# Attention with quantised heads before a routed expert block: sixteen small operations per tile moved from VectorE to GpSimd, and a ninth head written as bytes

## The chip, the cores and the metric

The kernel runs on one core of a Trainium2 chip. Its engines are TensorE (PE, the matrix engine), VectorE (DVE), ScalarE (ACT, activations such as the exponential), GpSimd (POOL) and SyncE (SP, which here only issues transfers). Each engine works through its own list of instructions in order; they wait for each other by semaphores. The metric is the device time of one execution in microseconds, the median of several.

## The reference

Two residual layers over x of 2 x 512 tokens with 512 channels. The first is cross attention to 2048 context rows with 16 heads of 32 channels, in which queries, keys, values and probabilities are rounded to whole numbers of a scale ("fake quantisation"):

```
q = (x @ Wq + bq) * scale ; k, v = split(cond @ Wkv + bkv)
q = _fq_sym(q, axis=-1) ; k = _fq_sym(k, axis=-1) ; v = _fq_sym(v, axis=2)
attn = softmax(einsum('bhqd,bhkd->bhqk', q, k), axis=-1)
attn = _fq_unsigned(attn, axis=-1)      # round(attn / (max/255)) * (max/255)
x = x + einsum('bhqk,bhkd->bhqd', attn, v) @ Wp + bp      # x was normalised before q
```

The second layer routes every token by a gate to some of 8 experts (a gated network each) and adds their weighted sum. The rounded probability of a key is round(255 * exp(s - max s)), a whole number from 0 to 255. The kernel computes just that: the exponential with the bias ln 255 - max s, written as an integer.

## The kernel before

**Stages.** Context rows, keys, values and queries are made and rounded first (to about 133 us). Then comes the attention over eight tiles i = 0 to 7 of 128 queries, each with 16 heads h; a position in it is written as "head h of tile i". A short tail follows (last projection, norm, gate, lists of tokens), then the experts. The change is all in the attention.

**One head** runs through the engines so:
- TensorE (`scores`) multiplies the queries with the 2048 keys, in two halves of 1024 in PSUM.
- VectorE *stages*: it multiplies with the negative step and writes to one of four `staged` buffers (h % 4), with the minimum of each row as an accumulated result. Even heads go in one operation over 2048 columns (`stage_whole`, L1258), odd heads in two over 1024 (`stage_half`, L1267). Then `make_bias` turns the minimum into the exponential's bias in `exp_bias`: for an even head `s_low + LN255` (L1278), for an odd one `min(s_low, s_first) + LN255` (L1276), 128 x 1 numbers each. In VectorE's list the bias of an odd head stands behind the whole staging of the next one, and the bias of an even head behind the first half of the next one.
- ACT takes the exponential (L946) of the staged scores. Even heads are written as bytes, odd heads as 16-bit words; the sum of the row comes along.
- SP issues a DMA transpose (L453), so that keys lie along the partitions. Of words that is 2048 columns; of bytes 1024, as two neighbouring bytes are turned as one 16-bit word.
- For a byte head POOL then takes the pairs apart (`unpack`, L632, a cast from bytes to 16-bit numbers). A word head needs nothing.
- TensorE multiplies with the values (`values`, L1639): in the slot of each even head h, heads h - 5 and h - 6.

**What sets the order.** Every engine's list is written out by hand. VectorE may stage a head when the exponential four heads before is done. ACT needs the bias, and for writing its result the transpose four heads before to have landed. An unpacking needs its transpose to have landed and the values of the head four before to be done.

**What else runs in a tile.** Between the heads stand: the attention result scaled and cut into two 16-bit parts by POOL (`attention_half`, L617 to L624) and transposed by SP (`transpose_attention`); the projection of the tile before by TensorE in four pieces at heads PROJECT_AT (L1521), which ACT takes at head 11 (L934) and POOL adds to x (`add_rows`, L639 to L643); the variance of the tile before that (L917 on ACT), its square root by nine small operations on POOL (`deviation`, L650 to L659), the normalised rows (L922, L928 on ACT, `rows_low` L664 on POOL), and their transpose and stores by SP (`store_rows`, `keep_rows`, `add_to_output`). POOL also copies the next queries into place (`next_queries`, L596). SP loads a piece of the expert weights per tile (`load_piece`). Where one of POOL's small operations needs the one before, it waits for its semaphore.

## Time and profile before

| | us |
|---|---|
| median of 3 runs | 745.07 (744.51 to 746.85) |
| the profiled execution | 742.73 |
| its span, first to last instruction | 740.9 |
| VectorE busy | 573.1 (77%) |
| ScalarE busy | 461.5 (62%) |
| GpSimd busy | 371.5 (50%) |
| TensorE busy | 623.8 (84%) |

The busy shares are means over stages with different limits, so they have to be read by stretches: the page cuts the span into 40 slices of 18.5 us. "Busy" counts instructions that compute; waits, register work and the issue of transfers aren't in it. A POOL instruction's row ends when its result is there; on VectorE and ACT the next instruction can start a little before the row of the last has ended.

### The profile page before, as it was taken

The page shows a single profiled execution, that of the slowest core. Times are in us where ns is not written, and L with a number is a line of the kernel's source. Part 1 is how long each engine was busy: PE and PEld are TensorE (multiplying, and loading weights), DVE is VectorE, ACT ScalarE, POOL GpSimd, SP SyncE. Part 2 cuts the span into 40 slices and gives each one's busy share as a digit, 9 for nine tenths or more (in the row PEclk, how much of TensorE's full clock was granted, in tenths as well). Part 3 has the DMA queues.
Part 4 walks back from the last instruction along what each step waited for, and adds up shares of the span by engine and source line. Part 5 has one row for each costly group of instructions (what it writes and reads, how often), then busy time and mean ns, then how long its engine had stood idle before and what let it go on. Part 6 is the DMA issues. An engine that isn't in the chain of part 4 may idle for free. (4 is left out here: it accounts for less than half of the span.)

```text
span 740.9 us, 15739 instructions
## 1 busy us (share of the span) xinstructions
PE 623.8 (84%) x5298; PEld 325.9 (44%) x5298; DVE 573.1 (77%) x974; ACT 461.5 (62%) x552; POOL 371.5 (50%) x394
## 2 busy tenths in 40 slices
PE   6999999566777777777767687799999999999993
PEld 2444443233434343343434355455555555555551
DVE  4997778999999999999999996784746537455330
ACT  6334358688899999999999997243434435344321
POOL 5254457544666675757576754215334453343503
PEclk9999999999999999999999999899999999999997
DMA  7767767999999999999999995459895887977804
GB/s 246 195 150 168 167 142 124 189 170 179 181 171 191 211 174 213 174 217 181 206 180 210 188 201 107 133 178 183 223 250 127 235 220 184 254 137 213 149 6 57
DMA packets 325908, 131.25 MB, mean 177 GB/s; under 512 B 300901, under 2 KB 300901, under 8 KB 325865
## 3 DMA queue, kind: packets, MB, share of 16 engines
q1 hardware_dynamic: 318688, 114.48, 71.5%
q0 software_dynamic: 7168, 16.26, 10.6%
q8 instruction: 19, 0.31, 0.2%
q14 instruction: 25, 0.20, 0.1%
q10 hardware_dynamic: 8, 0.01, 0.0%
HBM read 44.33 MB, written 12.06 MB: 76 GB/s over the span
## 5 line engine op out<-in xcount | busy, mean ns | idle before, releaser
L946 ACT ACTIVATE work<-spare,exp_bias 128x2048 int16<-128x2048 f32 (+1 forms) x128 | 255.5, 1996 | 32.0 <-DVE exp_bias L1276 30.4
L1267 DVE TENSOR_SCALAR_CACHE_REDUCE spare<-psum,q_step_now 128x1024 f32<-128x1024 f32 x128 | 162.2, 1274 | 0.1
L632 POOL CAST work<-work 128x2048 int16<-128x2048 uint8 x63 | 119.1, 1890 | 81.8 <-DMA work<-work 67.5
L1258 DVE TENSOR_SCALAR_CACHE_REDUCE spare<-psum,q_step_now 128x2048 f32<-128x2048 f32 x64 | 150.4, 2350 | 0.1
L1679 PE MATMUL psum<-keys_region,work 128*128 128x512 f16 x256 | 73.1, 383 | 52.1 <-DVE spare L1267 28.9
L1679 PE MATMUL psum<-keys_region,bias_hl 128*128 128x512 f16 x256 | 71.9, 382 | 32.1 <-DVE spare L1267 28.3
L737 POOL DMA_INDIRECT work<-x_rows,slot_tok x32 | 50.1, 1564 | 97.1 <-DVE slot_w L1453 73.8
L749 POOL DMA_INDIRECT out_dram<-keys_region,slot_tok x32 | 51.7, 1617 | 74.1 <-ACT keys_region L1025 67.1
L1521 PE MATMUL psum<-work,spare 128*128 128x480 f16 (+1 forms) x396 | 79.2, 360 | 0.9 <-DVE work L1426 0.9
L1521 PE MATMUL psum<-work,keys_region 128*128 128x480 f16 x384 | 78.9, 366 | 0.0
L1639 PEld LDWEIGHTS psum<-values_region,work 128*128 128x128 f16 x2048 | 67.4, 96 | 24.2 <-DMA work<-work 12.5
L1639 PE MATMUL psum<-values_region,work 128*128 128x32 f16 x2048 | 70.5, 176 | 3.6 <-DMA work<-work 3.4
L1475 DVE SCALAR_TENSOR_TENSOR resid<-resid,psum 128x480 f32<-128x480 f32 x32 | 20.7, 648 | 58.8 <-ACT resid L1015 58.8
L1679 PEld LDWEIGHTS psum<-keys_region,work 128*128 128x128 f16 x256 | 16.7, 97 | 95.8 <-DVE spare L1267 59.5
L1008 ACT ACTIVATE query_region<-resid 128x480 f16<-128x480 f32 x32 | 19.3, 603 | 61.3 <-DVE resid L1478 61.3
L1521 PEld LDWEIGHTS psum<-work,spare 128*128 128x128 f16 x396 | 38.3, 98 | 39.0 <-ACT work L1036 1.0
L1521 PEld LDWEIGHTS psum<-work,keys_region 128*128 128x128 f16 x384 | 37.3, 98 | 39.5
L1679 PEld LDWEIGHTS psum<-keys_region,bias_hl 128*128 128x128 f16 x256 | 17.9, 97 | 72.5 <-DVE spare L1267 57.9
L1025 ACT ACTIVATE keys_region<-psum,slot_w 120x512 f32<-120x512 f32 x32 | 21.2, 686 | 43.8 <-PE psum L1521 38.0
L1521 PE MATMUL psum<-query_region,work 128*128 128x512 f16 x192 | 44.8, 379 | 3.7 <-issue 2.8
L563 POOL TENSOR_TENSOR values_region<-values_region 128x512 f16<-128x512 f32 x16 | 21.6, 1349 | 50.1 <-ACT values_region L845 50.1
L1015 ACT ACTIVATE resid<-psum 128x480 f32<-128x480 f32 x32 | 18.2, 570 | 43.6 <-PE psum L1521 43.6
(222 smaller groups left out, 1014.0 us busy)
## 6 DMA issues: line engine op xcount, KB each, us to landing
spare<-in_L_ffn_Wd_dram SPq DMA_DIRECT2D x8, 1024.0 KB, 15.6
spare<-in_L_ffn_Wg_dram SPq DMA_DIRECT2D x7, 1024.0 KB, 5.7
spare<-in_L_ffn_Wu_dram SPq DMA_DIRECT2D x7, 1024.0 KB, 12.1
work<-in_ctx_dram SPq DMA_DIRECT2D x3, 1024.0 KB, 5.7
work<-work SPq DMA_TRANSPOSE x181, 3.6
token_region<-in_L_xattn_Wkv_dram SPq DMA_DIRECT2D x2, 1024.0 KB, 6.9
resid<-in_x_dram SPq DMA_DIRECT2D x2, 1024.0 KB, 8.7
x_rows<-work SPq DMA_DIRECT2D x8, 256.0 KB, 2.3
```

The lines of the kernel that those rows point to most:

```text
L563: nc.gpsimd.tensor_tensor(k_cut[b][:, :, 1, :], k_deq[b], k_cut[b][:, :, 0, :], ALU.subtract).then_inc(k_cut_ready[b], 1)
L632: nc.gpsimd.tensor_copy(p_T_int[h % 4 // 2], pair_bytes[h % 4 // 2]).then_inc(unpacked, 1)
L737: nc.gpsimd.indirect_dma_start(x_sel[par][:, t, :], None, x1_rows, bass.IndirectOffsetOnAxis(ap=slot_tok[par][:, t:t + 1], axis=0)).then_i ...
L749: nc.gpsimd.indirect_dma_start(out_rows, bass.IndirectOffsetOnAxis(ap=slot_tok[par][0:ROWS, t:t + 1], axis=0), y_out[0:ROWS, t, :], None, ...
L946: nc.scalar.activation(last_int[h % 2] if words and h >= H - 2 else p_int[h % 4], scores, ACT.Exp, bias=exp_bias[:, h % 4:h % 4 + 1], scal ...
L1025: nc.scalar.activation(y_out[0:ROWS, t, :], bank(4 + t % 3)[0:ROWS, :], ACT.Copy, scale=slot_w[par][0:ROWS, t:t + 1]).then_inc(y_ready[t % ...
L1258: nc.vector.tensor_scalar(staged[h % 4], psum[:, at:at + 4, :].rearrange("p b k -> p (b k)"), q_step_now[:, h:h + 1], None, ALU.mult, ALU.min,
L1267: nc.vector.tensor_scalar(staged[h % 4][:, 1024 * c:1024 * c + 1024], psum[:, at:at + 2, :].rearrange("p b k -> p (b k)"), q_step_now[:, h ...
L1475: own.link(nc.vector.scalar_tensor_tensor(gate_1[f % 2], tanh_g[f % 2], 1.0, bank(f % 2)[:, 0:PASS], ALU.add, ALU.mult))
L1521: ins = nc.tensor.matmul(out, lhs(a, c), rhs(b, c), start=start and n == 0, stop=stop and n == len(terms) - 1)
L1639: ins = nc.tensor.matmul(bank(6 + n)[:, at:at + HD], p_T[h % 4][:, t, :], v_int[:, t, h * HD:h * HD + HD], start=t == 0, stop=t == KT - 1)
L1679: ins = nc.tensor.matmul(bank(at + piece), q_now[h // HQ][:, h % HQ, :], key_parts[:, h // 2, 1024 * c + 512 * piece:1024 * c + 512 * piec ...
```

## The change

1. In tiles 1 to 7 the biases are made by POOL, head by head, as the first thing of each head's turn; only tile 0 and the last two heads of tile 7 stay with VectorE, under a semaphore of their own (`edge_bias`). VectorE's loop over the tiles 1 to 7 becomes tile 1, a loop over 2 to 6, and tile 7.
2. POOL's list for a tile is written anew around the biases: one other task between each two of them. The unpacking of head h - 3 follows the bias of the odd head h; the square root is done in two parts (after the biases 2 and 6).
3. Head 9 is written as bytes too (nine of sixteen heads, `BYTE_HEADS`), transposed in pairs and unpacked by POOL behind the bias of head 12. The buffers' views are made for all four places instead of two, and the counts of `unpacked` are 9 a tile.
4. ACT's work between the heads moves: normalising the rows from head 4 to 7, cutting them from 5 to 8, the squares from 13 to 15. In SP's list the first half of the attention is transposed at head 1 of the next tile instead of behind head 15, the second at 5 instead of 4; x1 is stored at head 2 and the rows at 10, where all three transfers stood at head 7; the weights' piece goes from 10 to 12.
5. PROJECT_AT goes from (8, 10, 10, 12) to (10, 10, 12, 12).
6. The semaphore `tri_ready` is merged into `const_ready`.

```diff
-PROJECT_AT = (8, 10, 10, 12)
+PROJECT_AT = (10, 10, 12, 12)
+BYTE_HEADS = (0, 2, 4, 6, 8, 9, 10, 12, 14)
...
             def transpose_tile(i, first, after_rows, count=H):
...
-                    if h == 10 and i < QT - 1 or first and h == 6:
+                    if h == 12 and i < QT - 1 or first and h == 6:
...
-                    if h == 4 and not first:
+                    if h == 1 and not first:
+                        transpose_attention(i - 1, 0)
+                    if h == 5 and not first:
                         transpose_attention(i - 1, 1)
-                    if h == count - 1:
+                    if h == count - 1 and count < H:
                         transpose_attention(i, 0)
-                    if h == 7 and after_rows:
+                    if h == 2 and after_rows:
+                        add_to_output(i - 2)
+                    if h == 10 and after_rows:
                         store_rows(i - 2)
...
+            def make_bias(i, h):
+                pool.wait_ge(scores_taken, 2 * H * i + 2 * h + 2)
+                passed()
+                at = slice(h % 4, h % 4 + 1)
+                if h % 2:
+                    nc.gpsimd.tensor_scalar(exp_bias[:, at], s_low[:, at], s_first[:, at], LN255, ALU.min, ALU.add).then_inc(bias_made, 1)
+                else:
+                    nc.gpsimd.tensor_scalar(exp_bias[:, at], s_low[:, at], LN255, None, ALU.add).then_inc(bias_made, 1)
...
             def attention_tile(i, after_rows, following):
...
+                if not following:
+                    add_at, half_at = 12, 13
+                else:
+                    add_at, half_at = 14, 15
+                for h in range(H if following else H - 2):
+                    make_bias(i, h)
+                    if h == 0:
+                        pool.wait_ge(unpacked, unpacked_earlier(i, 0))
+                        passed()
+                        next_queries(i, 1)
+                    if h == 1:
+                        unpack(i - 1, 14)
+                    if h == 2 and after_rows:
+                        scale = deviation_begun(i - 2)
+                    if h == 4:
+                        attention_half(i - 1, 1)
+                    if h == 6 and after_rows:
+                        deviation_ended(i - 2, scale)
+                    if h == 8 and following:
...
+                        next_queries(i + 1, 0)
+                    if h == 10 and after_rows:
+                        rows_low(i - 2)
...
+                    if h == 12:
+                        unpack(i, 9)
+                    if h % 2 and 3 <= h < 15:
+                        unpack(i, h - 3)
+                    if h == add_at:
+                        add_rows(i - 1)
+                    if h == half_at:
+                        attention_half(i, 0)
                 unpack(i, 12)
...
-                    words = h % 2 or not following and h == H - 2
+                    words = h not in BYTE_HEADS or not following and h == H - 2
...
-                    if h == 4 and after_rows:
+                    if h == 7 and after_rows:
                         normalise_rows(i - 2)
-                    if h == 5 and after_rows:
+                    if h == 8 and after_rows:
                         cut_rows(i - 2)
...
-                    if h == 13 and not first and following:
+                    if h == 15 and not first and following:
                         square_rows(i - 1)
...
-            def attention_tile(i, first):
+            def attention_tile(i, first, after_first=False, last=False):
                 for h in range(0, H, 2):
                     stage_whole(i, h, first)
-                    if h:
+                    if first and h:
                         make_bias(i, h - 1)
-                    elif not first:
-                        make_bias(i - 1, H - 1)
+                    if after_first and h == 0:
+                        make_bias(0, H - 1)
...
                     stage_half(i, h + 1, 0, first)
-                    make_bias(i, h)
+                    if first or last and h == H - 2:
+                        make_bias(i, h)
                     stage_half(i, h + 1, 1, first)
```

How the lists stand, in the instructions of the built programs. Lines are those of each program; `spare` holds the staged scores, `s_low` and `s_first` the minima, an operation over 2048 columns is a whole staging, one over 1024 a half, and REGISTER_ALU and ISA rows only work out what a wait compares with.

VectorE in a tile of the loop, before, a whole staging and the two halves behind it:

```order
L1258 TENSOR_SCALAR spare,s_low<-psum,q_step_now 128x2048
L1276 TENSOR_SCALAR exp_bias<-s_low,s_first 128x1
L1265 REGISTER_ALU
L1267 TENSOR_SCALAR spare,s_first<-psum,q_step_now 128x1024
L1278 TENSOR_SCALAR exp_bias<-s_low 128x1
L1265 REGISTER_ALU
L1267 TENSOR_SCALAR spare,s_low<-psum,q_step_now 128x1024
```

and the same place now:

```order
L1312 TENSOR_SCALAR spare,s_low<-psum,q_step_now 128x2048
L1301 REGISTER_ALU
L1319 REGISTER_ALU
L1321 TENSOR_SCALAR spare,s_first<-psum,q_step_now 128x1024
L1319 REGISTER_ALU
L1321 TENSOR_SCALAR spare,s_low<-psum,q_step_now 128x1024
```

Both biases are gone from it, and the stagings follow each other.

POOL in the second half of a tile of the loop, before: the unpacking of head 8, the rows added, the unpacking of head 10, and the attention's first half:

```order
L632 CAST work<-work 128x2048
L639 ISA
L639 TENSOR_TENSOR x_mean<-proj_sum,row_sum 128x1
L640 ISA
L640 TENSOR_TENSOR work<-work,resid 128x512
L75 ISA
L643 TENSOR_SCALAR x_mean<-x_mean 128x1
L630 REGISTER_ALU
L632 CAST work<-work 128x2048
L611 ISA
L614 REGISTER_ALU
L617 TENSOR_TENSOR work<-work,p_rsum 128x256
```

and now, from the bias of head 10 to the unpacking of head 8 behind bias 11 and that of head 9 behind bias 12:

```order
L659 TENSOR_SCALAR exp_bias<-s_low 128x1
L699 TENSOR_TENSOR work<-work 128x512
L653 REGISTER_ALU
L657 TENSOR_SCALAR exp_bias<-s_low,s_first 128x1
L645 REGISTER_ALU
L648 REGISTER_ALU
L650 CAST work<-work 128x2048
L653 REGISTER_ALU
L659 TENSOR_SCALAR exp_bias<-s_low 128x1
L648 REGISTER_ALU
L650 CAST work<-work 128x2048
```

Every task of POOL now has a bias ahead of it and one behind, and there is one unpacking more.

## Rows read from the trace of the kernel before

**Rows 1.** The page's slices: VectorE's busy tenths in 40 slices of 18.5 us.

```profile
DVE  4997778999999999999999996784746537455330
```

**Rows 2.** Busy us in one stretch: PE, its weight loads, DVE, ACT, POOL; clock, DMA.

```profile
289.00:328.00 39.00, 28.90 (x384) 15.60 (x384) 39.00 (x67) 35.74 (x44) 26.17 (x33) 1.00 0.98 194
```

**Rows 3.** VectorE in order of time: start, us, engine, line, operation, tiles.

```profile
307.58 1.28 DVE L1267 TENSOR_SCALAR_CACHE_REDUCE spare<-psum,q_step_now 128x1024 f32<-128x1024 f32 x1
...
308.78 2.35 DVE L1258 TENSOR_SCALAR_CACHE_REDUCE spare<-psum,q_step_now 128x2048 f32<-128x2048 f32 x1
...
311.05 0.22 DVE L1276 TENSOR_SCALAR exp_bias<-s_low,s_first 128x1 f32<-128x1 f32 x1
311.18 1.28 DVE L1267 TENSOR_SCALAR_CACHE_REDUCE spare<-psum,q_step_now 128x1024 f32<-128x1024 f32 x1
...
312.38 0.16 DVE L1278 TENSOR_SCALAR exp_bias<-s_low 128x1 f32<-128x1 f32 x1
312.44 1.28 DVE L1267 TENSOR_SCALAR_CACHE_REDUCE spare<-psum,q_step_now 128x1024 f32<-128x1024 f32 x1
...
313.64 2.35 DVE L1258 TENSOR_SCALAR_CACHE_REDUCE spare<-psum,q_step_now 128x2048 f32<-128x2048 f32 x1
...
320.90 0.20 DVE L1218 RECIPROCAL p_rsum<-p_sum 128x8 f32<-128x8 f32 x1
...
359.95 0.20 DVE L1218 RECIPROCAL p_rsum<-p_sum 128x8 f32<-128x8 f32 x1
```

**Rows 4.** POOL's groups from 250 to 406 us (four tiles), then rows by time.

```profile
L632 POOL CAST work<-work 128x2048 int16<-128x2048 uint8 x32 | 60.5, 1890 | 35.0 <-DMA work<-work 29.7 <-POOL bias_hl L596 2.0 <-PE psum L1639 1.4
...
L596 POOL COPY work<-query_region 64x512 f16 x8 | 4.9, 608 | 3.3 <-PE psum L1679 2.3 <-POOL work L596 1.0
...
L654 POOL TENSOR_SCALAR ln_t<-ln_y,ln_var 128x1 f32<-128x1 f32 x12 | 4.1, 341 | 2.5 <-POOL ln_y L655 1.7 <-POOL ln_y L651 0.8
...
L659 POOL TENSOR_SCALAR x_mean<-x_mean,ln_y 128x1 f32<-128x1 f32 x4 | 1.0, 260 | 0.4
...
305.13 0.62 POOL L617 TENSOR_TENSOR work<-work,p_rsum 128x256 f32<-128x256 f32 x1
...
307.10 1.89 POOL L632 CAST work<-work 128x2048 int16<-128x2048 uint8 x1
...
325.67 0.21 POOL L643 TENSOR_SCALAR x_mean<-x_mean 128x1 f32<-128x1 f32 x1
325.94 1.89 POOL L632 CAST work<-work 128x2048 int16<-128x2048 uint8 x1
```

**Rows 5.** ACT's exponentials in the same four tiles, and one by time.

```profile
L946 ACT ACTIVATE work<-spare,exp_bias 128x2048 int16<-128x2048 f32 x32 | 64.0, 2001 | 13.1 <-DVE exp_bias L1276 12.7
L946 ACT ACTIVATE work<-spare,exp_bias 128x2048 uint8<-128x2048 f32 x32 | 63.7, 1991 | 0.0
...
311.30 2.00 ACT L946 ACTIVATE work<-spare,exp_bias 128x2048 int16<-128x2048 f32 x1 [0.25 <-DVE exp_bias L1276]
```

**Rows 6.** SP's waits in four tiles; landing of one byte and one word head.

```profile
SPq L314 <- ACT work L946: 7.3, 13, 0.9
...
DMA to landing us min/median/max: 3.3/3.3/3.3
...
DMA to landing us min/median/max: 4.3/4.3/4.3
```

**Rows 7.** TensorE in the slot of head 10, tile 4, in order of time.

```profile
313.79 0.60 PE L1679 MATMUL psum<-keys_region,bias_hl 128*128 128x512 f16 x2 [0.66 <-DVE spare L1267]
...
315.26 1.50 PE L1521 MATMUL psum<-work 128*128 128x128 f16 x24
316.59 1.46 PE L1679 MATMUL psum<-keys_region,bias_hl 128*128 128x512 f16 x6
```

**Rows 8.** The tail by stretches; the figure behind the five engines is the granted clock.

```profile
447.90:451.30 3.40, 3.40 (x30) 2.80 (x28) 2.59 (x5) 3.10 (x6) 2.27 (x3) 0.51 0.85 199
...
471.80:475.20 3.40, 3.40 (x25) 1.68 (x24) 2.69 (x15) 0.00 (x0) 0.89 (x1) 0.50 0.00 0
```

134 lines of the change are left out of this document (69 added, 65 removed).

## Prediction, made before the changed kernel ran

> **What bounds the kernel now.** I read the page's slices first [rows 1]: VectorE is busy 9 tenths or more from slice 8 to slice 24, and that stretch, the attention over eight tiles of 128 queries, is where all edits lie. The table by stretches [rows 2] has VectorE busy for 39.00 us of every 39.00 us, ScalarE (ACT) 35.7, GpSimd (POOL) 26.2, TensorE 28.9. The same reciprocal of two tiles starts at 320.90 and 359.95 [rows 3]: one tile takes 39.05 us, and VectorE sets it. The chain of waits is of no use here; it names TensorE in the expert stage, which nothing touches. So the questions are what VectorE gives up, and who is next.
>
> Three others stand close behind. ACT sat idle for 13.1 us before the exponentials in four tiles [rows 5]: 3.3 a tile, so it needs 35.8. The SP queue waited 7.3 us in the same four tiles [rows 6]: 1.8 a tile, so it is occupied for 37.2. POOL waited 29.7 us for transposes to land and 2.3 + 1.4 for TensorE [rows 4], 8.35 a tile: what it must do takes 39.05 - 8.35 = 30.7, its own short gaps included.
>
> **VectorE: what it gives up.** The tile's biases stand in its stream twice per pair of heads. From one pair [rows 3]: the staging of the even head starts at 308.78, the bias L1276 at 311.05, the next staging at 311.18, the bias L1278 at 312.38, the staging behind it at 312.44. So a bias costs 0.13 us and 0.06 us from start to start, although the rows give 0.22 and 0.16 as their length, since the next instruction starts while it ends. Stagings that follow each other with no bias (312.44 to 313.64) already run in 1.20, so nothing else changes between them. Before, there are 128 biases; after, VectorE keeps the 16 of tile 0 and the last two of tile 7. 110 go, 55 of each kind: 55 x 0.13 + 55 x 0.06 = 10.45 us. A whole tile: 39.05 - 8 x 0.19 = 37.5.
>
> The rule that speaks of this price is in the Trainium skill, VectorE: DVE Perf Modes, section "The DRAIN you can't avoid": the next VectorE operation does not begin until the pipe is empty. Read so, each bias would cost its full row, and 55 x (0.22 + 0.16) = 20.9 us would go; the starts in the rows, which overlap the rows' ends, contradict it here.
>
> **GpSimd: what it takes on.** Per whole tile 16 biases and one more unpacking. A bias of an even head has the form of L643 (one operation with a constant), 0.21; one of an odd head that of L659 (a pointer and a constant), 0.260 [rows 4]. Behind such a short operation the next starts 0.06 us after its end (325.67 + 0.21 to 325.94 [rows 4]); I take 0.07. So 8 x 0.28 + 8 x 0.33 = 4.9. The unpacking of head 9 is a row of L632, 1.89. Sum: 30.7 + 4.9 + 1.9 = 37.5 us a tile, the same as VectorE's. The cover is gone: POOL has no spare time, and every wait in its stream is paid. A bound from below: the biases hide in their neighbours as on VectorE (0.13 and 0.06), which makes 34.1. From above: L654's 0.341 with its 0.21 of waiting for itself, 0.55 a bias, makes 41.4. I take the middle form since a bias waits for VectorE and not for POOL's own last result.
>
> A bias stands behind what POOL does for the head before. Longest is the turn of the tile: after bias 15, three operations of the attention's half (305.13 to 307.10, 2.0 [rows 4]) and an unpacking (1.9) stand ahead of bias 0, which then comes 4.2 us after bias 15 where the stagings come 2.3 apart: 1.9 late. Who waits: ACT's exponential of head 0. But an exponential may start late, as staging buffer h is taken again only four heads on: three intervals of 2.34 less the 2.0 of the exponential, 5.0 us. Today ACT starts it up to 2.4 us after the staging ended, since the bias of an odd head stands behind the next whole staging (half from 307.58, bias 311.05, exponential 311.30 [rows 3, 5]). POOL can be 2 us late and still be no later than now; per head it catches up some 0.1 to 0.2.
>
> The new wait: the unpacking of head h stands behind bias h + 3 and ahead of bias h + 4. It needs the exponential (2.0), the issue of the transpose and 3.3 us to its landing [rows 6]: 5.5 after bias h, against 7.0 for three heads. The spare 1.5 goes where ACT also norms and cuts the rows (heads 7 and 8) and POOL has no unpacking between two biases (head 10): there, for the unpackings of 8 and 9, I count 0.4 us of waiting a tile. So POOL's turn is 37.9, 0.4 over VectorE's for the five tiles 2 to 6: 1.9 us, of which tile 7 (no queries to fetch for a next one, 2 x 0.61 and their gaps [rows 4]) gives some back: **1.3 lost**. Bounds 0 and 3.
>
> **TensorE.** The projections move from heads 8, 10, 10, 12 to 10, 10, 12, 12: two slots with 24 small matmuls instead of one. In such a slot [rows 7] the 24 start at 315.26 and the scores behind them at 316.59; the first two of these six are through at about 316.59 + 1.46/3 = 317.08. VectorE's second half was started at 317.31 and would now be at 313.64 + 2.27 + 1.20 = 317.11. Nothing is left; I take 0.05 us in two slots of seven tiles: **0.7 lost**. Bounds 0 and 2.8 (0.2 a slot, by the 0.15 between a staging's end and the scores that it frees).
>
> **SP and ACT.** The issues stay as many; head 9's is half as large, the att transposes, the store of x1 and that of the rows are spread over heads 1, 2, 5, 10. SP's 37.2 becomes 37.2 less what a smaller transpose saves: the landing of a word head took 4.3 us from issue, that of a byte head 3.3, so up to 1 less. 36.2 to 37.2 fits under 37.9, hidden. ACT's exponential is as long for bytes as for words (1991 and 2001 ns), 35.8 fits too. Cost nothing, but with 0.7 and 1.7 us of cover left.
>
> **After the attention.** After the last exponential the tail (last probabilities, projection, norm, gate) and the experts shift as a whole. In the tail TensorE's granted clock falls to half for 3.4 us at 447.9, at 471.8 and once between [rows 8]. Where those stretches lie will change; TensorE is at the limit in about half of them, so 1.5 us either way, which I put into the range.
>
> **Sum.** -10.45 + 0.7 + 1.3 = -8.45 us. The profiled execution took 742.73 (span 740.9), 2.3 below the median of 745.07; its span would be 732.5. The time of the median kind: 745.07 - 8.45 = **736.6**.
>
> **Rivals.**
> - *GpSimd is the bound at a gain*: landings come later than counted, a turn of 38.5. Five tiles gain 0.55 each and the tiles 1 and 7 1 us each: 4.7 us less, 740.4 (738.5 to 743). For it: 37.5 is a sum of many short rows, and POOL cannot recover a wait. Against: before, the landings were ahead of it by 7.4 us a tile. Chance 0.20.
> - *Slower*: the same place, POOL between bias h + 3 and h + 4, above 39.05 us a tile. It decides from 1.5 us a tile more than my 37.5, which is 0.1 us on each bias or a 0.2 us wait at each of the nine unpackings. At 39.6 five tiles lose 0.55 each and the two others about 0.5: +3.3, 748.4. For it: the loop unpacking, bias, exponential, transpose, unpacking feeds back into itself. Chance 0.11. The Trainium skill, GPSIMD Engine Reference, section 4.1 "Engine selection", advises against it: two-input elementwise work is about twice as slow on GpSimd as on VectorE. With twice VectorE's rows (0.43, 0.31, and 0.07 each) the biases would cost 7.0 and the turn would be 39.6, this rival's number; the rows of like form (0.26 and 0.21 against 0.22 and 0.16) show 1.2 to 1.4 times.
> - *Nothing gained*: VectorE's 0.19 a pair turns into waiting for scores, as TensorE's order would be the bound: 745, within 0.3%. Against: between stagings TensorE waits for VectorE [rows 7], and a slot of the dear kind takes 4.3 us (313.79 to 318.05) of 4.67. Chance 0.07.
> - *Better than the sum*: no loss on POOL and TensorE and a good clock in the tail: 733 to 734. Chance 0.06.
> - The forecast itself, 734.5 to 738.5: 0.56.
>
> Faster by over 0.3% (2.2 us, about what a measurement of this kernel tells from no change): 0.56 + 0.06 + 0.16 of the first rival = 0.78. Slower by over 0.3%: 0.11. The rest, 0.11, within. The range 733.0 to 743.5 leaves out the slower rival and the edges.
>
> **What would show it.** Right: in tiles 2 to 6 the same reciprocal comes every 37.5 to 37.9 us; VectorE has no bias but staging after staging, idle under 0.5 us a tile; POOL is busy for about 33 of 37.7 us with waits for DMA below 1 us a tile. The first rival: VectorE idle on exponentials, POOL waiting for landings 1 us a tile. The third: VectorE idle on TensorE. Wrong altogether if the period falls and the span doesn't: then the tail took it back.

## The result, and the profile after

The changed kernel takes 749.46 us (median of 5 runs, 748.18 to 751.12), the kernel before on the same chip 744.79 (744.51 to 746.85): a ratio of 1.0061, 95% interval 1.0040 to 1.0082. It is slower by 0.6%, a small difference that the interval separates from none. 736.6 had been forecast, and 749.46 lies outside 733.0 to 743.5. Of the rivals the slower one happened: GpSimd (POOL) above 39.05 us a tile.

The profiled execution of the changed kernel has a span of 748.9 us, that of before 740.9. These 8.0 us lie between two single executions; the medians differ by 4.7. First a tile by stretches; the columns are those of [rows 2].

```profile
331.10:370.57 39.47, 28.25 (x384) 15.21 (x384) 37.92 (x53) 35.85 (x43) 32.52 (x50) 1.00 0.94 186
```

VectorE did give up its time: 37.92 busy of 39.47 us, where [rows 2] has 39.00 of 39.00. But the tile is longer. From the first staging of a tile to that of the next (on VectorE) tiles 0 to 6 took 40.61, 39.80, 38.75, 41.08, 38.36, 39.47 and 39.35 us; before, tile 0 took 38.86, tile 1 39.24 and the others 39.04 to 39.05. So the five middle tiles together are 1.8 us longer, and tile 0, in which VectorE still makes the biases, 1.75. These 1.75 can't be called a price of the change: with the same tile 0 experiment 2 and three of the four versions in experiment 10 took 38.86 for it, the fourth 40.18. Here TensorE's granted clock lay at half from 132.1 to 138.9 us. What VectorE waited for between 140 and 450 us (us in total, times, the longest):

```profile
DVE spare L1321 <- PE psum L1736: 9.4, 15, 1.5
DVE spare L1312 <- PE psum L1736: 2.5, 5, 0.5
```

It stood 11.9 us waiting for scores, more than the 10.45 us that its biases had cost. TensorE issues scores behind values, and waited in its turn for what the values need, and ACT for biases:

```profile
PE psum L1696 <- DMA work<-work: 19.6, 28, 2.0
...
ACT work L1000 <- POOL exp_bias L659: 13.7, 22, 1.8
ACT work L1000 <- POOL exp_bias L657: 13.5, 21, 1.1
PE psum L1696 <- POOL work L650: 9.4, 8, 1.8
```

One waiting leads to the next: staging waits for scores, these stand behind values, values wait for a landing or an unpacking, these come late since the exponential was late, and that waited for its bias on POOL. Here is POOL from one adding of the rows (L667) to the next, in order of time, answering to the rows by time in [rows 4]:

```profile
331.05 1.27 POOL L667 TENSOR_TENSOR work<-work,resid 128x512 f32<-128x512 f32 x1
...
339.13 0.30 POOL L657 TENSOR_SCALAR exp_bias<-s_low,s_first 128x1 f32<-128x1 f32 x1 [0.37 <-POOL bias_hl L614]
339.71 1.89 POOL L650 CAST work<-work 128x2048 int16<-128x2048 uint8 x1 [0.28 <-DMA work<-work]
...
344.01 0.30 POOL L657 TENSOR_SCALAR exp_bias<-s_low,s_first 128x1 f32<-128x1 f32 x1 [0.37 <-POOL ln_y L675]
344.37 1.89 POOL L650 CAST work<-work 128x2048 int16<-128x2048 uint8 x1
346.35 0.22 POOL L659 TENSOR_SCALAR exp_bias<-s_low 128x1 f32<-128x1 f32 x1
346.91 0.62 POOL L635 TENSOR_TENSOR work<-work,p_rsum 128x256 f32<-128x256 f32 x1 [0.34 <-ACT work L950]
...
365.75 1.89 POOL L650 CAST work<-work 128x2048 int16<-128x2048 uint8 x1
367.73 0.30 POOL L657 TENSOR_SCALAR exp_bias<-s_low,s_first 128x1 f32<-128x1 f32 x1
368.09 1.89 POOL L650 CAST work<-work 128x2048 int16<-128x2048 uint8 x1
...
370.51 1.27 POOL L667 TENSOR_TENSOR work<-work,resid 128x512 f32<-128x512 f32 x1
```

From 331.05 to 370.51 are 39.46 us; I call this POOL's turn. The two waits for another engine or a transfer that it shows (0.28 and 0.34) are all there are in it. So POOL's own work with its own gaps is 38.9 us a turn, where the forecast had 37.5. The unpackings (1.89) and the stagings (2.35 and 1.27) are as long as before, so POOL's added work does not lengthen VectorE's operations, nor its own. A bias is 0.30 or 0.22 long, and four of the eight odd ones stand 0.36 to 0.37 us behind a result of POOL's own.

The attention's last exponential starts later too. First the kernel before, then the changed one:

```profile
447.29 1.99 ACT L946 ACTIVATE work<-spare,exp_bias 128x2048 int16<-128x2048 f32 x1
```

```profile
452.58 2.00 ACT L1000 ACTIVATE work<-spare,exp_bias 128x2048 int16<-128x2048 f32 x1 [0.38 <-DMA work<-work]
```

5.3 of the 8.0 us between the two spans are lost by here; 2.7 more behind it. The latter is no clear price of the change either: from the last exponential to the end it took 293.6 us before and 296.3 here, and 293.7 to 297.8 in the other versions below, none of which alters anything there. In the tail TensorE's granted clock lay at half (1.2 of 2.4 GHz) for 13.6 us in one piece, answering to the separate 3.4 us of [rows 8]:

```profile
470.00:483.60 13.60, 11.72 (x95) 6.12 (x94) 10.30 (x46) 2.56 (x5) 2.25 (x3) 0.50 0.19 67
```

### The profile page after: what moved, and what is told of

It reads as the page before. It is cut to its first block, busy times and chain, and to the rows that moved or that the text cites. A ratio compares the mean times of both kernels' runs of the same rounds, so it can differ in the third digit from the quotient of the medians.

```text
span 748.9 us, 15883 instructions
## 1 busy us (share of the span) xinstructions
PE 630.3 (84%) x5298; PEld 328.7 (44%) x5298; DVE 566.1 (76%) x864; ACT 462.1 (62%) x552; POOL 419.9 (56%) x512
## 4 chain that ended last, share of the span: by engine, by line
PE 50%; issue 15%; DMA 8%; DVE 7%; SPq 7%; ACT 5%; POOL 5%; POOLq 1%; another core or an unknown queue 1%; ACTq 0%; DVEq 0%
PE psum L1578 45%; DMA work<-work 8%; ACT work L1000 4%; SPq L467 3%; DVE spare L1321 2%; POOL work L650 2%; SPq L435 2%; SPq L465 2%; DVE spare L1312 1%; PE psum L1583 1%; PE psum L1793 1%; PE psum L1875 1%; PE psum L1787 0%; POOL exp_bias L657 0%
## 5 line engine op out<-in xcount | busy, mean ns | idle before, releaser
L1000 ACT ACTIVATE work<-spare,exp_bias 128x2048 uint8<-128x2048 f32 (+1 forms) x128 | 255.5, 1997 | 37.0 <-POOL exp_bias L659 13.7
L1321 DVE TENSOR_SCALAR_CACHE_REDUCE spare<-psum,q_step_now 128x1024 f32<-128x1024 f32 x128 | 160.3, 1273 | 9.6 <-PE psum L1736 9.4
L650 POOL CAST work<-work 128x2048 int16<-128x2048 uint8 x71 | 134.2, 1892 | 27.8 <-DMA work<-work 15.7
L783 POOL DMA_INDIRECT work<-x_rows,slot_tok x32 | 52.6, 1644 | 97.7 <-DVE slot_w L1510 73.0
L1736 PE MATMUL psum<-keys_region,work 128*128 128x512 f16 x256 | 76.6, 411 | 34.6 <-DVE spare L1321 19.2
L1696 PE MATMUL psum<-values_region,work 128*128 128x32 f16 x2048 | 71.3, 177 | 32.6 <-DMA work<-work 22.6
L1696 PEld LDWEIGHTS psum<-values_region,work 128*128 128x128 f16 x2048 | 65.9, 96 | 61.1 <-DMA work<-work 41.0
L1578 PEld LDWEIGHTS psum<-work,keys_region 128*128 128x128 f16 x384 | 37.3, 98 | 39.5
L1736 PEld LDWEIGHTS psum<-keys_region,work 128*128 128x128 f16 x256 | 19.3, 102 | 77.6 <-DVE spare L1321 47.1
L1736 PEld LDWEIGHTS psum<-keys_region,bias_hl 128*128 128x128 f16 x256 | 19.4, 98 | 59.2 <-DVE spare L1321 44.4
```

What stands on the lines that cost most here:

```text
L650: nc.gpsimd.tensor_copy(p_T_int[h % 4], pair_bytes[h % 4]).then_inc(unpacked, 1)
L783: nc.gpsimd.indirect_dma_start(x_sel[par][:, t, :], None, x1_rows, bass.IndirectOffsetOnAxis(ap=slot_tok[par][:, t:t + 1], axis=0)).then_i ...
L1000: nc.scalar.activation(p_out, scores, ACT.Exp, bias=exp_bias[:, h % 4:h % 4 + 1], scale=-1.0, accum_out=p_sum[:, h:h + 1]).then_inc(exp_do ...
L1321: nc.vector.tensor_scalar(staged[h % 4][:, 1024 * c:1024 * c + 1024], psum[:, at:at + 2, :].rearrange("p b k -> p (b k)"), q_step_now[:, h ...
L1578: ins = nc.tensor.matmul(out, lhs(a, c), rhs(b, c), start=start and n == 0, stop=stop and n == len(terms) - 1)
L1696: ins = nc.tensor.matmul(bank(6 + n)[:, at:at + HD], p_T[h % 4][:, t, :], v_int[:, t, h * HD:h * HD + HD], start=t == 0, stop=t == KT - 1)
```

## Experiments

Diffs are against the changed kernel. "Turn" is the time between two starts of L667 in the middle tiles.

**1. Nine unpackings halved.** From tile 1 on POOL unpacks only one byte of each pair (the rest of the conversion is left out).

```
-nc.gpsimd.tensor_copy(p_T_int[h % 4], pair_bytes[h % 4])
+nc.gpsimd.tensor_copy(p_T_int[h % 4][:, 0:1], pair_bytes[h % 4][:, 0:1])   # tile 0: whole
```

> The changed kernel, but from tile 1 on each unpacking takes apart only one byte of each pair (half the columns), so the probabilities of every second block of keys are stale; all else is the same. POOL's work falls by about 8 x 0.9 = 7 us a tile. Theory P (POOL's own work of about 39 us a tile sets the pace of tiles 2 to 6 in the changed kernel, through late biases, late exponentials and late values): a tile takes 37.5 to 37.9 us, the waits of VectorE for scores nearly vanish, and the time is 9 to 14 us below the changed kernel's 749.5, 736 to 741. Theory S (the two slots with 24 projection matmuls hold the scores up): the waits before the second halves of heads 11 and 13 stay at 0.6 us each, a tile takes 38.7 or more, the time falls by under 3 us. Theory C (the new order of SP's and ACT's work): also under 3 us.

Measured: 734.78 us, ratio to before 0.9893 (0.9858 to 0.9927), turn 37.7 to 37.9. One tile by stretches:

```profile
320.00:357.80 37.80, 28.61 (x393) 15.80 (x389) 37.78 (x51) 35.73 (x43) 24.83 (x49) 1.00 0.99 195
```

VectorE is busy throughout, at 37.8 us: the forecast's 37.5 and a little. The two slots of TensorE with two projections cost nothing when the values are there on time. With POOL relieved the change is worth what it was meant to be (0.9893, where 736.6 against 745.07 is 0.9886), so the loss comes through POOL. The edit does two things at once, though: it takes 7.6 us of work from POOL, and it brings every byte head's values 0.85 us nearer to its landing. It can't tell POOL's load from the length of that way; experiments 4 and 7 bear on it.

**2. All biases back on VectorE**, in the changed layout, with head 9 as bytes.

```
 # VectorE, each tile (the odd heads' biases and ACT's waits likewise)
-                    if first or last and h == H - 2:
-                        make_bias(i, h)
+                    make_bias(i, h)
...
 # POOL, each head
-                    make_bias(i, h)
```

> The changed kernel's order on SP, ACT, POOL and TensorE and nine byte heads, but all biases on VectorE where they stood before. VectorE's need is 39.05 us a tile again, POOL's about 39.1 less 16 biases of 0.37 to 0.45, 32 to 33. Theory P: 39.05 a tile and no waits, 743.5 to 746, equal to before. Theories S and C (order or slots cost by themselves): slower than before, 747 to 752, with VectorE waiting for scores, and TensorE's clock falling inside the attention.

Measured: 744.43, ratio 1.0018 (1.0004 to 1.0032), turn 39.0 to 39.1. So the new order and the ninth byte head cost 0.2% by themselves at a VectorE that needs 39.05 us a tile; that they would cost as little at one that needs 37.5 is not shown by this run. Most of the loss came with the biases on POOL. In two turns POOL waited here:

```profile
POOL work L650 <- DMA work<-work: 9.3, 12, 1.5
POOL work L635 <- ACT work L949: 2.9, 2, 1.5
POOL work L650 <- PE psum L1689: 1.4, 3, 0.5
...
POOL bias_hl L614 <- PE psum L1729: 1.1, 2, 0.5
POOL work L614 <- PE psum L1729: 0.9, 2, 0.4
```

15.6 us in two, 7.8 a turn. To take all of this off (39.07 - 7.8 = 31.3) would be too much, because a part of it is there without any waiting for others. First a copy of queries and two unpackings in this run:

```profile
333.15 0.61 POOL L614 COPY bias_hl<-query_region 64x512 f16 x1 [0.54 <-PE psum L1729]
...
336.02 1.89 POOL L650 CAST work<-work 128x2048 int16<-128x2048 uint8 x1 [1.42 <-DMA work<-work]
...
340.15 1.89 POOL L650 CAST work<-work 128x2048 int16<-128x2048 uint8 x1 [0.50 <-POOL ln_y L675]
```

and the places of the first two before (the third row is the unpacking behind the other copies):

```profile
333.74 0.61 POOL L596 COPY bias_hl<-query_region 64x512 f16 x1 [0.45 <-POOL work L632]
...
335.71 1.89 POOL L632 CAST work<-work 128x2048 int16<-128x2048 uint8 x1 [0.51 <-POOL bias_hl L596]
...
354.37 1.89 POOL L632 CAST work<-work 128x2048 int16<-128x2048 uint8 x1 [0.42 <-POOL work L596]
```

The copy that waited 0.54 for TensorE stands 0.45 behind POOL's own unpacking anyway, and of the 1.42 for a landing 0.51 would be there too. Behind such results of POOL's own the two first copies and the two unpackings behind the copies stand 0.36 to 0.51 each, 1.7 us a turn, and the list waits for one more (L699) that no run here shows free of another wait. So POOL's own work without biases is about 33.0 us, 33.4 with the same 0.4 at L699. Sixteen biases bring it to 38.9: 5.5 to 5.9 us, 0.34 to 0.37 each. This is an estimate from these rows; whole waits taken off would give 7.6 us or 0.47 each.

**3. The projections at their old heads**, `PROJECT_AT = (8, 10, 10, 12)`.

> The changed kernel with the projections at heads 8, 10, 10, 12 as before. Theory S: the wait before the second half of head 13 goes, that of head 11 stays; 0.6 us a tile, 745 to 746. Theory P: the slot of head 8 has no slack for values that come late either, so the wait moves there; within 1.5 us of 749.5, or slower.

Measured: 768.16, ratio 1.0343 (1.0318 to 1.0368). VectorE waited 13.0 us for TensorE in 157 us, less than four of the turns of 42.4 to 42.8, and TensorE for the transposed attention:

```profile
DVE spare L1321 <- PE psum L1736: 13.0, 4, 4.3
...
PE psum L1578 <- DMA work<-work: 9.5, 3, 3.3
```

Since the second transpose of the attention now stands behind head 5, the first projection comes too early at head 8. The move was needed; it says nothing on the price of the double slots.

**4. Head 9 as words again**: `BYTE_HEADS` without 9, and its unpacking gone from POOL, 2 us a turn.

> The changed kernel with head 9 written as words again (eight byte heads, no unpacking behind bias 12), all else as changed. By theory P it takes 1.89 + 0.4 us off POOL's turn of about 39.1: 36.8 a tile, under VectorE's 37.5; a tile takes 37.5 to 38.0 and the time is 737 to 742, better than both kernels, unless the larger transpose (SP and DMA) takes its place: then 744 to 748 with POOL waiting for landings over 1 us a tile. Theory S: within 2 us of 749.5.

Measured: 748.28, ratio 1.0073 (1.0047 to 1.0098), turn 39.5 to 39.9. POOL was relieved of a whole unpacking and nothing came back. In four tiles it waited for the values of earlier heads, and 3.2 us for landings:

```profile
POOL work L650 <- PE psum L1692: 5.6, 3, 1.9
```

A tile:

```profile
331.10:370.80 39.70, 28.58 (x389) 15.19 (x388) 37.94 (x51) 35.85 (x44) 30.46 (x49) 1.00 0.97 192
```

POOL is busy for 30.46 us here, 2 less than in the changed kernel, and the tile is no shorter. So POOL's load alone does not set the turn.

**5. Head 9 as words and the other unpackings halved.**

> As the run with head 9 as words, and GpSimd unpacks only one byte of each pair from tile 1 on (this part of the probabilities' conversion is left out). GpSimd is then far from the bound. Theory D (with head 9 as words the transposes take 38.4 us of DMA time a tile, against 37.3 with it as bytes, and with the waits around them they are the next bound): tiles of 38.5 to 39.0 us, 740 to 744. Theory P alone (only GpSimd's work counts): as with nine byte heads, 37.8 us a tile, 734 to 737.

Measured: 740.24, ratio 0.9926 (0.9902 to 0.9951). A tile:

```profile
323.81:362.02 38.21, 28.98 (x384) 15.57 (x384) 37.76 (x51) 35.64 (x43) 23.77 (x48) 1.00 1.01 199
```

The DMA engines are busy all the time (1.01): with eight byte heads their transfers need about 38.2 us a tile, with nine (experiment 1) under 37.8. This bound stands in [rows 2] too, as the last but one figure, 0.98 of 39.00 us, and the prediction didn't use it. With eight byte heads it would have held the tile near 38.2 us, above VectorE's 37.5. The turn of experiment 4 lies 1.3 to 1.7 above 38.2, so this bound by itself doesn't explain that run.

**6. More throwaway matmuls**: four instead of two behind the values of each odd head, to see if the half clock inside the attention is a cause.

> The changed kernel with four instead of two throwaway matmuls behind the values of each odd head, so that TensorE waits less idly. Theory C (the stretches of 3.4 us at half clock inside the attention are a cause of the longer tiles): these stretches go or become rarer, tiles near 39.0, 744 to 747. Theory P (they are a consequence of waiting for GpSimd): 748 to 751, and the tiles stay at 39.4 in the mean or above, with the stretches at half clock or without.

Measured: 749.88, ratio 1.0052 (1.0033 to 1.0072), five stretches at half clock between 160 and 400 us as before. The filling came behind the wait, not into it, so this shows only that two more matmuls there neither help nor hurt.

**7. One unpacking halved, at four places.** A half unpacking takes 1.04 instead of 1.89 us, so the relief is 0.85 us a turn. Only the head differs:

```
+whole = slice(0, 2) if isinstance(i, int) and i == 0 or h != 9 else slice(0, 1)
-nc.gpsimd.tensor_copy(p_T_int[h % 4], pair_bytes[h % 4])
+nc.gpsimd.tensor_copy(p_T_int[h % 4][:, whole], pair_bytes[h % 4][:, whole])
```

> The changed kernel with the unpacking of head 9 alone cut to one byte of each pair from tile 1 on (that part of the conversion is left out): GpSimd is relieved by 0.95 us a tile, a ninth of what the run with all nine cut was relieved by. Theory P: slope one, tiles of 38.5 instead of 39.5 us, 742 to 744. If GpSimd's work were only one of several causes, or the loop of late landings the main one: 746 to 749.

> The changed kernel with the unpacking of head 4 alone cut to one byte of each pair from tile 1 on (that part of the conversion is left out). Same relief of GpSimd as in the run that cut head 9's, 0.95 us a tile, but at another place of its turn: head 4 is unpacked behind bias 7, where the exponentials' lag behind the stagings still climbs to its highest value at heads 8 and 9, head 9 behind bias 12, where it falls anyway and GpSimd only waits for the next landing sooner. Theory W (what counts is GpSimd's work between the turn of the tile and the peak of the lag): tiles of 38.4 to 38.8 us and 742 to 745.5, at least 2 us under the run that cut head 9's. Theory P in its simple form (GpSimd's sum over a tile counts, wherever it lies) and theory C (the half clock): the same as that run, 747 to 749.

> The changed kernel with the unpacking of head 0 alone cut to one byte of each pair from tile 1 on (that part of the conversion is left out): again 0.95 us a tile less for GpSimd, now behind bias 3, ahead of the biases 4 to 7. Theory R (rings: GpSimd's work of 38.9 us a tile is tied within some tenths with a path bias 7 - exponentials 7 to 10 - landing of head 10 - its unpacking, and with the SP queue, whose transposes of heads 2 to 6 follow each other without a pause): only a part comes back, a turn of 38.9 to 39.3 us and 743.5 to 746.5, ratio to before 1.001 to 1.005, better than both others since this place lies ahead of bias 7. If GpSimd's work alone decided: 38.5 us and 741 to 743. If nothing of so small a relief came back: 39.4 and 746 to 748.

> The changed kernel with the unpacking of head 2 alone cut to one byte of each pair from tile 1 on (that part of the conversion is left out): 0.95 us a tile less for GpSimd, as at heads 9, 4 and 0, now behind bias 5, where no path through ScalarE runs beside it. Theory R (one ring holds the turn at 39.4: bias 3 - exponential 3 - ScalarE's taking of the attention - GpSimd's half - bias 5 - bias 7 - exponentials 7 to 10 - landing of head 10 - unpacking - bias 15 - half - bias 0 - bias 3; the heads 0, 4 and 9 lie beside ScalarE's stretches of it, head 2 lies on it): the relief counts in full, a turn of 38.4 to 38.8 us, 742.5 to 745.5 where the kernel before takes 745, ratio 0.997 to 1.001. If a relief of this size is lost wherever it lies: 39.4 us, ratio 1.003 to 1.006.

| halved head | ratio to before (95%) | turns in tiles 3 to 5, us |
|---|---|---|
| none (changed kernel) | 1.0061 (1.0040 to 1.0082) | 39.42, 39.59, 39.46 |
| 9 | 1.0032 (1.0013 to 1.0050) | 39.04, 39.45, 39.43 |
| 4 | 1.0052 (1.0039 to 1.0065) | 39.17, 39.42, 39.40 |
| 0 | 1.0034 (1.0021 to 1.0047) | 39.26, 39.50, 39.48 |
| 2 | 1.0030 (1.0016 to 1.0044) | 39.18, 39.31, 39.35 |

Little of the 0.85 comes back, at no place: at most 0.4 us in a turn, mostly under 0.2. Over the six turns between the first and the last L667, 0.7 to 1.3 us of 5.1 come back. In each trace POOL stands at the next operation that needs another engine's result. Head 9 (the short unpacking, then the wait for head 10's landing):

```profile
363.12 1.04 POOL L651 CAST work<-work 128x1024 int16<-128x1024 uint8 x1
364.25 0.30 POOL L658 TENSOR_SCALAR exp_bias<-s_low,s_first 128x1 f32<-128x1 f32 x1
365.30 1.89 POOL L651 CAST work<-work 128x2048 int16<-128x2048 uint8 x1 [0.75 <-DMA work<-work]
```

Head 4, with the wait at the unpacking of head 6 (with head 2 halved it is 0.94 at the same place):

```profile
355.85 1.89 POOL L651 CAST work<-work 128x2048 int16<-128x2048 uint8 x1 [0.98 <-DMA work<-work]
```

Head 0, with the wait at the attention's half, for ACT's copy that follows exponential 3:

```profile
344.90 1.04 POOL L651 CAST work<-work 128x1024 int16<-128x1024 uint8 x1
346.02 0.22 POOL L660 TENSOR_SCALAR exp_bias<-s_low 128x1 f32<-128x1 f32 x1
347.44 0.62 POOL L635 TENSOR_TENSOR work<-work,p_rsum 128x256 f32<-128x256 f32 x1 [1.20 <-ACT work L951]
```

In the changed kernel POOL stands 0.06 to 0.34 us at the same places. So POOL's work is tied, within a few tenths, with the way from a bias over the exponential and the transpose (or ACT's copy) back to POOL, at several places of the turn. My theory of one place that counts (heads ahead of bias 7) fell with head 0 and again with head 2.

**8. Heads 2 and 12 halved.**

> The same with the unpacking of head 12 (behind the turn of the tile, ahead of bias 0) cut too: both lie on the ring of theory R, 1.9 us a tile. The ring would need 37.5, so VectorE's 37.5 to 37.8 us and the DMA engines' 37.3 hold the tile: 37.8 to 38.2 us, 737.5 to 741, ratio 0.990 to 0.995, as much as the run with all nine unpackings cut reached, with two. If lost wherever it lies: 39.0 us or more, ratio above 1.000.

Measured: 0.9987 (0.9973 to 1.0002), turns of 38.60, 38.64 and 38.52. Against head 2 alone that is 0.6 to 0.8 less a turn, 4.6 us over the six: the second relief, at head 12's unpacking ahead of bias 0 of the next tile, gave back most of its 0.85. Head 12 was not halved alone, so whether its place did it, or the two reliefs together, is not shown. The forecast of 37.8 to 38.2 failed here too.

**9. The SP queue.** First the second transpose of the attention halved besides head 4's unpacking (the low halves are not transferred):

```
-att_T[:, DK * n:DK * n + DK, :], att_hl[:, n].rearrange("p l d -> p (l d)")      # kept for n = 0 and tile 0
+att_T[:, DK * n:DK * n + DK // 2, :], att_hl[:, n, 0]
```

> As the run that cut head 4's unpacking, and besides the second of the two transposes of the attention rows in each tile moves only the high halves (half the bytes; the low halves are left out of the transfer). It stands in the SP queue between the transposes of heads 5 and 6 and takes the queue 1.8 us. Theory R: the 0.95 us that GpSimd gained there was lost in waiting for head 6's landing behind this transpose; now it comes back: a turn of 38.5 to 38.9 instead of 39.4 us, 741 to 744. If the SP queue has no part in it: as the run with head 4 alone, 39.4 us and 745 to 747.

Measured: 1.0036 (1.0023 to 1.0050), turns 39.20, 39.24, 39.42. Against head 4 alone at most 0.2 us less: missed. But it doesn't test the queue. The halved transpose occupied it for 1.74 us at the place where the whole one took 1.62 in the run with head 4 alone (over the tiles a median of 1.68, against 1.64 for the whole transposes of both halves): half the bytes went, the queue's time stayed. Then two transfers of 256 KB moved behind head 8, where the queue has pauses:

```
-                    if h == 12 and i < QT - 1 or first and h == 6:
+                    if h == 8 and i < QT - 1 or first and h == 6:
 ...
-                    if h == 2 and after_rows:
+                    if h == 8 and after_rows:
                         add_to_output(i - 2)
```

> The changed kernel with two 256 KB transfers of the SP queue moved to behind the transpose of head 8, where the queue has pauses: the weights' piece (from behind head 12) and the output's store (from behind head 2). In the trace of the changed kernel the queue issues without a pause from head 10 of a tile to head 5 of the next, and both transfers lie in that stretch, 1.1 us of issuing and the transfers' own time. Theory R (the turn of 39.4 us is held by a ring over bias 7, the exponentials 7 to 10, the SP queue from head 10 to head 14, the landing of head 14, its unpacking behind bias 1): the ring gets 1 us shorter and GpSimd's own 38.9 to 39.1 us is left: 745 to 747.5, ratio to before 1.000 to 1.004. If the SP queue is no part of the bound: 748 to 751, 1.004 to 1.008.

> The same two moves of the SP queue, and the biases of heads 2, 5, 6 and 14 on VectorE. Theory R: GpSimd's own work is down to 37.9 us, VectorE's to 37.8 and the ring over the SP queue is 1 us shorter: a turn of 38.0 to 38.5 instead of the 38.9 us without the moves, 738 to 742, ratio 0.991 to 0.996, the fastest so far. If the SP queue is no part of the bound: as without the moves, 38.9 us, 743 to 746, ratio 0.997 to 1.000.

Measured: 1.0095 (1.0072 to 1.0117) with a turn of 40.2 to 40.5, and with four biases on VectorE 1.0040 (1.0023 to 1.0057). Both worse than without the moves, and both forecasts missed. The two transfers delay the landing of head 9:

```profile
368.82 1.89 POOL L650 CAST work<-work 128x2048 int16<-128x2048 uint8 x1 [1.21 <-DMA work<-work]
```

The pauses behind head 8 were not spare: what was issued there, heads 9 and 10, was already on the path.

**10. Fewer biases on POOL.** Even heads on VectorE; heads 0 to 7; heads 0, 2, 4, 6, 8; heads 2, 5, 6, 14. The first:

```
 # POOL
+                    if h % 2:
                         make_bias(i, h)
 # VectorE (ACT's waits are counted accordingly)
-                    if first or last and h == H - 2:
-                        make_bias(i, h)
+                    make_bias(i, h)
```

> The changed kernel with the biases of the even heads (the cheap kind for VectorE: 0.06 us from start to start) back on VectorE, and only those of the odd heads (0.13 us there) on GpSimd. Theory P (GpSimd's own work of 38.9 us a tile is the bound of the changed kernel): GpSimd gives up 8 x 0.29 us and needs 36.6, VectorE needs 39.05 - 8 x 0.13 = 38.0, so tiles of 38.0 to 38.4 us, seven of them, and 737.5 to 740.5. Theory C (what costs is any bias that goes through GpSimd, since its unpackings stand ahead of it in the queue, or the half clock of TensorE): tiles of 39.0 us and more, 744 to 749.

> The changed kernel with the biases of heads 0 to 7 on VectorE (4 x 0.13 + 4 x 0.06 = 0.76 us a tile) and those of heads 8 to 15 on GpSimd. Theory W: GpSimd is relieved by 8 x 0.33 = 2.6 us, all of it in the part where the lag climbs; the lag stays under 3.5 us, VectorE is the bound at 37.5 + 0.76 = 38.3 to 38.5 us in every tile: 739 to 742, as good as the split by even and odd heads or up to 2 us better, since no tile shows VectorE waiting for TensorE. Theory C: 743 to 748.

> The changed kernel with the biases of heads 0, 2, 4, 6 and 8 on VectorE (5 x 0.06 = 0.3 us a tile) and the other eleven on GpSimd (relief 5 x 0.29 = 1.45 us, all in the climbing part). Theory W: VectorE at 37.5 + 0.3 = 37.8 us is nearly the bound, the lag peaks near 4 us: tiles of 37.9 to 38.4, 737 to 741, the fastest of these versions. If GpSimd's sum decides (38.9 - 1.45 = 37.5, and its waits on top, 38.5 or more): 742 to 745.

> The changed kernel with the biases of heads 2, 5, 6 and 14 on VectorE (0.31 us a tile by the rows of before). In the traces so far the biases of heads 0, 4, 8 cost GpSimd nothing, as the next operation waits 0.36 to 0.45 us for the unpacking ahead of them anyway; those of 2, 6 and 14 cost 0.3 each, that of 5 costs 0.37. Theory R: GpSimd's turn 39.4 - 1.2 = 38.2 to 38.7 us, VectorE at 37.8: 738.5 to 742, at least as good as the two splits with eight biases on VectorE. If those are the best there is because VectorE takes eight: 743 to 746.

| biases on VectorE | us | ratio to before (95%) | turns, us |
|---|---|---|---|
| 0, 2, 4 ... 14 | 743.64 | 0.9975 (0.9956 to 0.9993) | 38.50, 38.71, 38.58 |
| 0 to 7 | 740.59 | 0.9972 (0.9957 to 0.9987) | 39.48, 38.70, 38.28 |
| 2, 5, 6, 14 | 744.75 | 0.9982 (0.9963 to 1.0002) | 38.77, 38.96, 38.84 |
| 0, 2, 4, 6, 8 | 744.10 | 1.0024 (1.0011 to 1.0037) | 39.14, 39.22, 39.22 |

(Medians of different chips; the ratios compare.) The first two beat both kernels, by 0.25 to 0.28% against before, less than forecast by the ratio (the 740.59 us of the second lie inside its 739 to 742, but on a chip where the kernel before takes 742.74). The second met its forecast of the tile: on VectorE four of its tiles 2 to 6 took 38.45 us or 38.46, the fifth 39.43. The last two missed theirs. In the first, VectorE is the bound again in a quiet tile:

```profile
326.00:364.34 38.34, 28.63 (x384) 15.50 (x384) 38.20 (x59) 35.20 (x42) 30.32 (x42) 1.00 0.96 190
```

Its POOL is busy for 30.32 us, as in experiment 4, and yet its tile is 1.4 us shorter: again POOL's load alone does not set it. Experiment 4 differs also in head 9's larger transpose, with the DMA engines busy for 0.97 of 39.70 us against 0.96 of 38.34; how much of the 1.4 is theirs was not separated.

In the last, five biases gone from POOL brought 0.2 to 0.4 us. One reason is in its rows, where bias 0 is gone between an unpacking and the copy of queries:

```profile
331.64 1.89 POOL L650 CAST work<-work 128x2048 int16<-128x2048 uint8 x1
333.97 0.61 POOL L614 COPY bias_hl<-query_region 64x512 f16 x1 [0.45 <-POOL work L650]
```

The copy waits for the unpacking's own semaphore and starts 0.45 us behind its end; in the changed kernel, with the bias in between, the same copy starts 0.45 us behind it too (334.97 + 1.89 to 337.31 in its trace). That bias was free. And the two turns from 288.55 us hold 3.0 us of waiting for landings, ACT's copy and issues, so POOL's own work is 39.2 - 1.5 = 37.7 a turn: nearly the forecast's 37.5, and the turn is 39.2 all the same. The trace shows a second reason, tiles of 40.2 and 40.5 us between tiles of 38.1 and 38.2. Two stretches at the end of a long one:

```profile
322.50:325.90 3.40, 1.70 (x36) 1.09 (x36) 3.40 (x5) 3.40 (x8) 3.10 (x5) 1.00 1.03 222
325.90:329.30 3.40, 3.40 (x16) 1.08 (x13) 2.45 (x5) 3.40 (x3) 3.14 (x6) 0.50 1.13 212
```

TensorE, busy for half of the first stretch, among other things because it waited for an unpacking (1.17 us at one point), gets half its clock in the second; VectorE then stands for 0.95 of 3.40 us. The stretches at half clock end each long tile in this trace. Here the half clock is part of the loss: late values leave TensorE idle, the clock falls, scores come later still. The changed kernel has five such stretches between 160 and 400 us, the kernel before none, those of experiments 1 and 2 and the first two of this table one each. So they go with the waiting; that they follow from it is read from rows like these. No run took the half clock away by itself, so how much of the changed kernel's loss is theirs is open.

## Why the prediction was wrong, step by step

- **VectorE's 10.45 us: right.** 37.5 us a tile was forecast, 37.8 is seen where VectorE is busy throughout (experiment 1), so 1.25 of the forecast 1.5 us came back; with eight even biases it is busy for 38.2. Prices from start to start (0.13 and 0.06) held within 0.3 us a tile; the row lengths would have given 36.0.
- **POOL's turn, 37.5 and 0.4 of waiting: the step that failed, in both terms.** Its own work is 38.9, 1.4 more than the sum. By the estimate of experiment 2 the base is 33.0 to 33.4, not 30.7 + 1.9 = 32.6. The 8.35 of waits that I took off contain gaps of POOL's own (its copies among the 2.3 for TensorE), and the square root in two parts adds one, 0.50 at 340.15 in that run. The biases cost 5.5 to 5.9, not 4.9: 0.34 to 0.37 each and not 0.31. I took the gap around a bias as 0.07 from one pair of rows [rows 4]; measured it is 0.08 to 0.10 ahead of most, and an odd bias is 0.298 long, not 0.260. Four stand 0.36 to 0.37 behind a result of POOL's own, but most of that gap is no price of theirs: without the bias the unpacking stands 0.42 to 0.51 at three of these places. The slower rival's threshold was 1.5 us a tile over 37.5; the turn of 39.46 lies 2.0 over it, 1.4 in work and 0.6 in waits.
- **The waiting counts as much as the sum.** Even with a right 37.5 the turn would not have been 37.9: with POOL's own work at 37.7 (experiment 10, the last) it is 39.2, with 1.5 us of waits where 0.4 had been put, and with a whole unpacking less (experiment 4) it is 39.5 to 39.9.
- **"POOL can be 2 us late": too generous.** I had counted 5.0 us of room between staging and exponential and a catching up of 0.1 to 0.2 a head. In tiles 2 to 7 the exponentials of heads 5 to 10 started 3 to 5.3 us behind the staging's end, where before it was 2.2 to 2.7, and VectorE stood for scores. The lag only falls from head 9 on.
- **TensorE's 0.7: wrong as to cause.** The double slots cost nothing in experiment 1 (0.3 us of waiting for scores from 209 to 440 us). But VectorE waited 11.9 us for scores, since they stand behind values in TensorE's list. The third rival had that symptom; the cause was POOL.
- **SP and ACT "cost nothing": wrong.** Busy time fitted, latency did not. The feedback that I gave only to the slower rival (unpacking, bias, exponential, transpose, unpacking) held more widely: in the traces of experiments 7 and 9 what POOL gains or is given goes into waits for landings and ACT's copy. And the share of the DMA engines, 0.98 in [rows 2], was a bound that I read past.
- **Tail: right in kind, too small in size.** 1.5 us either way had been allowed; in the profiled execution it lost 2.7, with 13.6 us at half clock in one piece. Experiment 2 has such a piece as well, so it doesn't come from the biases, and the other versions' tails spread over 4 us.
- **The rule weighed there.** GPSIMD Engine Reference, section 4.1 "Engine selection", in the Trainium skill, advises against elementwise work on GpSimd, about twice as slow with two inputs and roughly level with one; the forecast set against the factor of two the row lengths (1.2 to 1.4 times). From start to start the factor here is larger than both: 0.34 to 0.37 a bias on POOL against (0.13 + 0.06) / 2 = 0.095 on VectorE, nearly 4 times. The rule's direction was right. That the turn worked out by it, 39.6, came near the measured 39.46 is in part luck: its biases were 1.1 to 1.5 too dear, its base 0.4 to 0.8 too cheap, and the measured turn holds 0.6 of waits that it had not.
- **Open:** which path holds the turn at 39.3 to 39.5 us when POOL has 0.85 us less to do. Four trials at single places and two moves in the SP queue refuted each single path that I named; the queue with less to do was never tried, as the halved transpose took it just as long. That several lie within a few tenths of each other fits all of them but was not tested as such, and only two reliefs together (experiment 8) gave back most of the second.

## What to carry to other kernels

Count work that is moved to another engine from start to start at its new place, and take off what would stand there anyway. Here a bias was free in a gap of 0.45, and took 0.45 (365.75 + 1.89 to 368.09 in the changed kernel) between two unpackings. When a wait is taken off to find an engine's own work, look how long it stands there when nobody else is late. Before giving an engine its last spare time, look whether its results come back to it through other engines; if they do, its waits before the change were not spare but the slack of that loop. And read the DMA share of a stretch as a bound like any engine's.

## What the runs showed of the hardware

- On GpSimd a bias starts 0.08 to 0.10 us behind an operation that the list does not wait for. Behind a result of GpSimd's own that it waits for, the next operation starts 0.17 to 0.25 us later where this is the only wait (the steps of the square root, the second copy), 0.36 to 0.45 with a second wait for another engine long satisfied (biases, the first copy), 0.42 to 0.51 with two such (an unpacking). That the number of waits is the cause is my reading.
- A bias of 0.22 put into the gap of 0.45 between an unpacking and the copy that waits for it costs nothing.
- Half the elements of the unpacking take 1.04 instead of 1.89 us. A DMA transpose of half the bytes (experiment 9) occupied the issuing queue as long as the whole: 1.68 against 1.64 us in the median.
- One stretch at half clock inside the attention goes with 0.95 us of standing on VectorE while it lasts.
